# A cross-attention and quantised feed-forward kernel: GpSimd's additions wait for the affine passes, and the weight preparation moves from VectorE to ScalarE and GpSimd

## Chip, cores and metric

The kernel runs on one core of a Trainium2 chip. The metric is the device time of one execution, in microseconds. Engine names: PE or TensorE (matmuls), DVE or VectorE, ACT or ScalarE, POOL or GpSimd, SP or SyncE (DMA issue only here).

## What is computed

The input x is [64, 256, 256], the context [64, 120, 192], all float32. For each of the 64 blocks:

```python
x = x + xattn(layernorm(x), ctx, Wq, Wk, Wv, Wo, bo)      # 8 heads of 32
x = x + ffn(layernorm(x), ln1_g, ln1_b, w1, b1, ln2_g, ln2_b, w2, b2)

def ffn(x, ...):
    h = layernorm(x, ln1_g, ln1_b)
    h = bitlinear(h, w1, b1)          # 256 -> 1024
    h = gelu(h)
    h = layernorm(h, ln2_g, ln2_b)
    return bitlinear(h, w2, b2)       # 1024 -> 256

def act_quant_fake(x):                # per row
    scale = 127.0 / clip(max(abs(x), axis=-1), 1e-5)
    return clip(round(x * scale), -128, 127) / scale
def weight_quant_fake(w):             # per matrix
    scale = 1.0 / clip(mean(abs(w)), 1e-5)
    return clip(round(w * scale), -1, 1) / scale
def bitlinear(x, w, b):
    return act_quant_fake(x) @ weight_quant_fake(w).T + b
```

## The kernel before

The work has two stages over the same 64 blocks of 256 rows (NB = 64, two tiles of 128 rows each). The first does attention, the residual, the first feed-forward norm and its quantising, and keeps the quantised rows in SBUF. The second does the feed-forward part. Nothing of the second stage is changed.

Each engine has one program, written out by hand, and all follow the same step counter i. In the first stage a step of an engine is its function `attn(i, n)`, called by `steps`: steps from A0 = -5 up to L0 = 24 are straight code, those from 24 to 55 run in a hardware loop that holds four steps, the rest is straight again. After a straight step, and only there, `steps` calls what the table `aside` holds for it. Different parts of a step work on different blocks: the scores on block i, the values and sums on block i-1, the projection and the residual on i-2, the affine pass and the quantising on i-3.

What matters of a step, in each engine's own order:

- TensorE: scores (L1242), values (L1269), sums (L1278), first half of the projection (L1324), the turning of the score maxima (`turn_minima`, L1249), second half of the projection (L1324), `first_values` (L1288), the shift of the scores (L1255), `keys` (L1293 to L1298, behind x1_done), queries (L1314), `spread_inverses` (L1305).
- VectorE: the two affine passes of block i-3 (L702, `h = h * f_r + b1n_bc`, one for each row tile, both inputs in SBUF; then h_affine goes up), the transposing maximum of the scores in PSUM (L691, nm_part), the largest magnitude of h (L713), L718, L723, L729 (nm_t), the projection added to x (L735, x1_done), the reciprocals L739 (h_scaled) and L744, statistics (L749), L757 (inv_part), L762, the centring of h (L767, two) with f_ve between them (L771), the scaling of the queries (L779), the weighing of the output (L788). Its `aside` comes after L788.
- GpSimd: a wait for the scores of step i (raw_ps, released by L1242), the bias b2 added to xr of block i-3 (`add_b2`, L490), bo added to xr of block i-1 (`add_bo`, L485), three small operations of the input norm (L515, L517, and the power L520, which makes x_r), the quantising of block i-3 (`quantise`: L496 and twice L498, behind h_scaled), and the power L528 that makes f_r for the next affine passes (behind f_ve). Its `aside` comes after L528.
- ScalarE: copies of keys and values (L994, L996), a copy of the output (L977), four passes for the input statistics (L1009, L1013), the exponentials (L988), L982, and the cast of the quantised rows (L972). Its `aside` comes last.
- SP issues the DMAs in a fixed order, each behind the semaphore of what it needs: the turning of h (L382), ctx_t, xt, x_in, r_rows (behind r_done), xr, the store of xr (behind b2_done) and r_bc (behind the landed r_rows).

The weights are prepared in the same steps through `aside` (W_STEP = 4). SP loads w1 and w2 in eight pieces at steps 4 to 11. VectorE splits the bias b1 into three bf16 parts at steps 8 to 11 (`split_bias`: casts L655, subtractions L659, on one partition with 1024 elements), sums the magnitudes of the weights at steps 12 to 15 (`magnitude`, L635, four of 128x1024), makes mean and inverse at step 16 (L640 to L643, after TensorE's sum over partitions), and clamps at steps 18 to 21 (`clamp_weight`, L649, four of 128x1024). GpSimd rounds at steps 17 and 18 (`round_weight`, L463, two of 128x2048). ScalarE casts to bf16 at steps 19 to 22 (`place_weight`, L964, four of 128x1024). SP stores the bias parts at step 13 (`store_bias`, L355) and loads them back as rows at step 14 (`place_bias`, L361). At steps 57 and 58 VectorE inverts the scales of the quantised rows (`invert_scales`, L664, L666), and at steps 58 and 59 GpSimd splits them (`split_scales`).

## Time and profile before

| | us |
|---|---|
| median of 3 runs | 1240.67 |
| the runs | 1234.32, 1240.67, 1245.86 |
| the profiled execution's own time | 1247.94 |
| its span in the profile | 1246.3 |
| mean granted TensorE clock | 0.96 of full |

All durations below come from that one profiled execution. Its span runs from the first to the last instruction; the 1.6 us between it and the execution's own time lie around it. A line number stands for a line of the kernel before. Busy time of an engine counts instructions, not waiting; "idle before" is the time in which an engine had nothing to do ahead of an instruction, and the arrow names what released it. GpSimd's spans are rough, and the ends of matmuls are modelled. Steps are counted by the maximum L691, of which there is one for each block.

### The profile page before, as it was taken

Reading aid. Unit: us, or ns where it says so; the run is one execution under the profiler, and the core shown is the slowest. Engines: PE = TensorE matmul, PEld = TensorE weight load, DVE = VectorE, ACT = ScalarE, POOL = GpSimd, SP = SyncE. Lnnn points to the kernel's source line nnn. Section 1 sums busy time; section 2 is a strip of 40 time slices with the busy share of each in tenths; the row PEclk is TensorE's granted clock in tenths of the full one; section 3 lists DMA queues with packets and bytes.
Section 4 is the critical chain, followed back from the end, with each engine's and each line's share of the span. In section 5 each row is a group of like instructions: output and inputs, shape, how many; then the busy total and the mean of one; then the engine's idle time right before and its main releaser. Section 6 shows DMA issues by size and latency. Waiting matters only on the chain.

```text
span 1246.3 us, 29490 instructions
## 1 busy us (share of the span) xinstructions
PE 1007.4 (81%) x9649; PEld 671.1 (54%) x9649; DVE 1139.0 (91%) x1719; ACT 812.8 (65%) x2083; POOL 715.0 (57%) x924
## 2 busy tenths in 40 slices
PE   5988887888888888889888976777777777777776
PEld 4666655555666666666665643444444444444444
DVE  2799988889999999999999898999999999999997
ACT  4555544455545555555554447699999999999994
POOL 3355644545545555555555543767766766776776
PEclk8999988889999999999999887899999999999998
DMA  5467854445655655565656340032233223223224
GB/s 149 134 144 161 161 121 115 113 97 120 126 127 135 134 137 132 137 139 131 126 135 138 79 104 26 18 43 34 34 38 38 34 34 42 34 34 38 37 34 68
DMA packets 144472, 114.63 MB, mean 92 GB/s; under 512 B 51580, under 2 KB 134908, under 8 KB 144408
## 3 DMA queue, kind: packets, MB, share of 16 engines
q1 hardware_dynamic: 126824, 96.90, 34.4%
q0 software_dynamic: 16864, 16.26, 10.4%
q8 instruction: 36, 0.59, 0.2%
q10 hardware_dynamic: 720, 0.66, 0.2%
q14 instruction: 28, 0.23, 0.1%
HBM read 71.75 MB, written 33.63 MB: 85 GB/s over the span
## 4 chain that ended last, share of the span: by engine, by line
DVE 47%; PE 25%; issue 23%; POOL 3%; DVEq 1%; DMA 1%; ACT 0%; POOLq 0%; ACTq 0%
DVE nm_part L691 11%; PE banks L1314 10%; DVE h L702 8%; DVE gn_low L815 6%; DVE gn_high L815 6%; PE banks L1324 4%; PE banks L1293 4%; DVE o_t L788 3%; DVE xr L735 3%; DVE gn_high L801 2%; PE banks L1295 2%; POOL gn_high L541 1%; DVE gn_low L801 1%; DVE q_t L779 1%; PE banks L1297 1%
## 5 line engine op out<-in xcount | busy, mean ns | idle before, releaser
L988 ACT ACTIVATE probs<-banks 120x512 f32<-120x512 f32 x256 | 138.8, 598 | 206.2 <-PE banks L1255 206.2
L691 DVE TRANSPOSE_TENSOR_REDUCE nm_part<-banks 128x64 f16<-128x2048 f32 x64 | 147.4, 2304 | 4.7 <-PE banks L1242 4.6
L1324 PE MATMUL banks<-wo_sb,o_t 128*128 128x256 f32 x512 | 149.6, 418 | 0.9 <-DVE o_t L849 0.9
L1026 ACT ACTIVATE g_dev<-g,g_sum 128x1024 bf16<-128x1024 f32 x128 | 149.1, 1165 | 0.0
L1031 ACT ACTIVATE g<-banks,h_dq 128x1024 f32<-128x1024 f32 x128 | 142.5, 1131 | 7.4 <-PE banks L1189 7.4
L490 POOL TENSOR_TENSOR xr<-xr,b_bc 128x512 f32<-128x512 f32 x64 | 98.4, 1537 | 63.6 <-PE banks L1242 63.6
L1207 PE MATMUL banks<-w_t,g_t 128*128 128x256 bf16 x1008 | 123.2, 276 | 12.8 <-ACT g_t L1064 11.1
L1314 PE MATMUL banks<-xt,wq_c 128*128 128x256 f32 x512 | 130.6, 399 | 0.0
L1183 PE MATMUL banks<-w_t,h_t 128*128 128x512 bf16 x512 | 125.9, 390 | 1.9 <-ACT g L1031 1.3
L1207 PEld LDWEIGHTS banks<-w_t,g_t 128*128 128x128 f16 x1008 | 94.8, 99 | 51.4 <-issue 29.8
L702 DVE SCALAR_TENSOR_TENSOR h<-h,f_r,b1n_bc 128x256 f32<-128x256 f32 x122 | 115.8, 990 | 0.1
L528 POOL TENSOR_TENSOR f_r<-f_ve,neg_half 128x2 f32<-128x2 f32 x62 | 49.5, 798 | 110.6 <-DVE f_ve L771 110.6
L1314 PEld LDWEIGHTS banks<-xt,wq_c 128*128 128x128 f32 x512 | 94.0, 193 | 18.8 <-issue 0.9
L1324 PEld LDWEIGHTS banks<-wo_sb,o_t 128*128 128x128 f32 x512 | 91.2, 198 | 22.0 <-issue 14.0
L485 POOL TENSOR_TENSOR xr<-xr,bo_bc 128x512 f32<-128x512 f32 x64 | 91.5, 1430 | 17.0 <-DMA xr<-in_x 17.0
L496 POOL COPY h_dq<-h_cl 128x2 f32<-128x2 f32 (+1 forms) x64 | 13.9, 216 | 148.9 <-DVE h_qs L739 147.8
L561 POOL TENSOR_TENSOR g_r<-g_ve,neg_half 128x2 f32<-128x2 f32 x64 | 91.4, 1428 | 10.3 <-ACT g_ve L1047 10.3
L536 POOL TENSOR_TENSOR g_dq<-g_max,w_out 128x2 f32<-128x2 f32 x64 | 12.2, 190 | 146.1 <-DVE gn_low L815 85.7
L1249 PE MATMUL banks<-ident_h,nm_part 128*128 128x128 f16 x64 | 14.1, 221 | 95.2 <-DVE nm_part L691 95.2
L994 ACT ACTIVATE k_t<-banks 128x256 f32<-128x256 f32 x64 | 24.6, 385 | 99.9 <-DVE q_t L779 99.9
L1201 PE MATMUL banks<-ident_h,gn_low 128*128 128x128 f16 x512 | 42.0, 229 | 54.3 <-POOL gn_low L541 54.3
L801 DVE SCALAR_TENSOR_TENSOR gn_low<-g,g_nm,g_bc 128x1024 f32<-128x1024 f32 x64 | 81.3, 1277 | 0.0
(166 smaller groups left out, 2774.9 us busy)
## 6 DMA issues: line engine op xcount, KB each, us to landing
x_in<-in_x SPq DMA_DIRECT2D x64, 256.0 KB, 3.6
xt<-in_x_t SPq DMA_DIRECT2D x64, 256.0 KB, 3.5
xr<-in_x SPq DMA_DIRECT2D x64, 256.0 KB, 5.5
out<-xr SPq DMA_DIRECT2D x64, 256.0 KB, 5.7
out<-res POOLq DMA_DIRECT2D x62, 256.0 KB, 4.2
ctx_t<-in_ctx_t SPq DMA_DIRECT2D x64, 128.0 KB, 2.9
r_bc<-r_rows SPq DMA_DIRECT2D x64, 128.0 KB, 4.1
w_raw<-in_w_t SPq DMA_DIRECT2D x8, 256.0 KB, 5.2
```

Of the source, the lines that this page charges most:

```text
L490: pool.tensor_tensor(xr[:, r, :, :], xr[:, r, :, :], b2_bc[:, :].unsqueeze(1).to_broadcast([P, T, D]), ALU.add).then_inc(b2_done, 1)
L691: dve.tensor_reduce(nm_part[:, :, 0:C * RB], blocks_p, AX.X, ALU.max, negate=True, apply_transpose=True).then_inc(max_done, 1)
L702: last = dve.scalar_tensor_tensor(out=h[:, r1, t, :], in0=h[:, r1, t, :], scalar=f_r[:, q, t:t + 1], in1=b1n_bc[:, :], op0=ALU.mult, op1=A ...
L801: dve.scalar_tensor_tensor(out=gn[n][:, t, :], in0=g[:, p, t, :], scalar=g_nm[:, p, t:t + 1], in1=g2_bc[:, :], op0=ALU.add, op1=ALU.mult). ...
L815: dve.scalar_tensor_tensor(out=gn[n][:, t, :], in0=gn[n][:, t, :], scalar=g_r[:, p, t:t + 1], in1=b2n_bc[:, :], op0=ALU.mult, op1=ALU.add) ...
L988: act.activation(probs[:, p, j, :, :], sc_p[0:KV, j, :, :], ACT.Exp, scale=SCALE).then_inc(probs_done, 1)
L1026: act.activation(g_dev[:, t, :], g[:, p, t, :], ACT.Square, scale=-float(F), bias=g_sum[:, p, t:t + 1], accum_out=g_ssq[:, p, t:t + 1]).th ...
L1031: act.activation(g[:, p, t, :], u_p[t], ACT.Gelu, scale=h_dq[:, b, t:t + 1], accum_out=g_sum[:, p, t:t + 1]).then_inc(gelu_done, 1)
L1183: pe.matmul(u_p[t][:, cols], h_t[:, b, t * C + c, :], w1_t[:, c, cols], start=(c == 0), stop=False, skip_group_check=True)
L1207: pe.matmul(y[t], turned_rows[:, t, f, :], w2_t[:, f, :], start=(first and f == 0), stop=False, skip_group_check=True)
L1314: last = pe.matmul(q_p[:, m, :], wq_c[:, c, m * P:(m + 1) * P], xt[:, p, c, :], start=(c == 0), stop=(c == C - 1))
L1324: last = pe.matmul(y_p[:, t, :], o_t[:, p, c, t * P:(t + 1) * P], wo_sb[:, c, :], start=(c == 0), stop=(c == C - 1))
```

## The change

- On GpSimd, the wait for the scores at the head of a step is gone; `add_b2` of block i-3 now waits for h_affine of that block, which VectorE raises after the second pass L702.
- `magnitude` moves from VectorE to ScalarE, at the same steps 12 to 15: an Abs activation with a running sum. Its elementwise result goes to w1_t or w2_t, which `place_weight` writes over later.
- Rounding and clamping are both on GpSimd, in eight passes over 128x1024, alternating, one in each of the steps 18 to 25. They stand inside `attn`, between `quantise` and the power L528. `place_weight` comes at steps 20, 22, 24 and 26.
- The bias b1 lies on 128 partitions with 8 elements each for the split; its load and the three stores have pieces of 8 elements.
- L0, the first looped step, is 28.

```diff
@@ -285,8 +285,8 @@
         ctx_t = sb("ctx_t", [P, 2, 2, KP], scope=early_mem)
         w1_raw = sb("w1_raw", [P, C, F], scope=early_mem)
         w2_raw = sb("w2_raw", [P, FC, D], scope=early_mem)
-        b1_row = sb("b1_row", [1, F], scope=early_mem)
-        b1_part = sb("b1_part", [1, 3, F], BF16, scope=early_mem)
+        b1_cols = sb("b1_cols", [P, F // P], scope=early_mem)
+        b1_part = sb("b1_part", [P, 3, F // P], BF16, scope=early_mem)
         wq_sb = sb("wq_sb", [P, C, D], scope=early_mem)
         early_mem.close()
         ffn_mem = ctx.enter_context(ExitStack())
@@ -323,7 +323,7 @@
         biast_p = bank[3][:, 512 - P:512]
         u_p = [pair_a.rearrange("p a n -> p (a n)"), pair_b.rearrange("p a n -> p (a n)")]
 
-        A0, L0, L1 = -5, 24, NB - 5
+        A0, L0, L1 = -5, 28, NB - 5
         FFN_L0, FFN_L1, FFN_END = 8, NB - 3, NB + 3
         N_CONST = 7 + C * T
         SPLIT = (0, (NB - 12) // 2, NB - 12, NB)
@@ -341,7 +341,7 @@
                         sp.dma_start(dst[:, :], src.rearrange("(a n) -> a n", a=1).to_broadcast([P, D])).then_inc(rows_load, 16)
 
                 def load_bias():
-                    sp.dma_start(b1_row[:, :], b1.rearrange("(a n) -> a n", a=1)).then_inc(b1_load, 16)
+                    sp.dma_start(b1_cols[:, :], b1.rearrange("(p n) -> p n", p=P)).then_inc(b1_load, 16)
 
                 def load_weight(n):
                     part = slice(n % 4 * F * C // 4, (n % 4 + 1) * F * C // 4)
@@ -352,8 +352,8 @@
                 def store_bias():
                     sp.wait_ge(s_b1, 4)
                     for row, parts in ((0, 3), (3, 2), (5, 1)):
-                        sp.dma_start(b1_rows[row:row + parts].rearrange("(a r) n -> a (r n)", a=1),
-                                     b1_part[0:1, 0:parts, :].rearrange("a r n -> a (r n)")).then_inc(bias_stored, 16)
+                        sp.dma_start(b1_rows[row:row + parts].rearrange("r (p n) -> p r n", p=P),
+                                     b1_part[:, 0:parts, :]).then_inc(bias_stored, 16)
 
                 def place_bias():
                     sp.wait_ge(bias_stored, 16 * 3)
@@ -457,10 +457,23 @@
                 def bias_here():
                     pool.wait_ge(s_load, 16 * 2)
 
-                def round_weight(m):
-                    raw = (w1_raw, w2_raw)[m]
+                def weight_part(n):
+                    m, part = n // 2, n % 2
+                    raw = (w1_raw, w2_raw)[m][:, :, :].rearrange("p a n -> p (a n)")[:, part * C * F // 2:(part + 1) * C * F // 2]
+                    return m, raw
+
+                def round_weight(n):
+                    m, raw = weight_part(n)
                     pool.wait_ge(mean_done, 2)
-                    pool.tensor_scalar(raw[:, :, :], raw[:, :, :], w_inv[:, m:m + 1], MAGIC, ALU.mult, ALU.add).then_inc(w_rounded, 1)
+                    pool.tensor_scalar(raw, raw, w_inv[:, m:m + 1], MAGIC, ALU.mult, ALU.add).then_inc(w_rounded, 1)
+
+                def clamp_weight(n):
+                    m, raw = weight_part(n)
+                    pool.wait_ge(w_rounded, n + 1)
+                    pool.tensor_scalar(raw, raw, MAGIC + 1.0, MAGIC - 1.0, ALU.min, ALU.max).then_inc(w_clamped, 1)
+
+                weight_steps = {W_STEP + 14 + 2 * n: (lambda n=n: round_weight(n)) for n in range(4)}
+                weight_steps.update({W_STEP + 15 + 2 * n: (lambda n=n: clamp_weight(n)) for n in range(4)})
 
                 def split_scales(m):
                     v = slice(SPLIT[m], SPLIT[m + 1])
@@ -478,7 +491,6 @@
                     pool.tensor_copy(bias_row[:, v, :, 5], h_res2[:, v, :]).then_inc(split_chain, 1)
 
                 aside = {-1: bias_here, 1: lambda: pool.wait_ge(rows_load, 16 * 3), NB - 6: lambda: split_scales(0), NB - 5: lambda: split_scales(1)}
-                aside.update({W_STEP + 13 + n: (lambda n=n: round_weight(n)) for n in range(2)})
 
                 def add_bo(b, r):
                     pool.wait_ge(xr_loaded[r], (b - r) * 4 + 16)
@@ -501,10 +513,9 @@
 
                 def attn(i, n):
                     p, q = n % 2, 1 - n % 2
-                    if live(i, NB) and live(i - 1, NB):
-                        pool.wait_ge(raw_ps, i + 1)
                     b = i - 3
                     if live(b, NB):
+                        pool.wait_ge(h_affine, b + 1)
                         add_b2(b, (n + 1) % 4)
                     b = i - 1
                     if live(b, NB):
@@ -521,6 +532,8 @@
                     b = i - 3
                     if live(b, NB):
                         quantise(b, (n + 1) % 4)
+                    if isinstance(i, int) and i in weight_steps:
+                        weight_steps[i]()
                     b = i - 2
                     if live(b, NB):
                         after(pool, h_affine, b - 1)
@@ -628,13 +641,6 @@
                 def rows_here():
                     dve.wait_ge(rows_load, 16 * 3)
 
-                def magnitude(n):
-                    m, part = n // 2, n % 2
-                    dve.wait_ge(w_load, 16 * 8)
-                    w = (w1_raw, w2_raw)[m][:, :, :].rearrange("p a n -> p (a n)")
-                    dve.tensor_reduce(w_abs[:, part, m:m + 1], w[:, part * C * F // 2:(part + 1) * C * F // 2], AX.X, ALU.add,
-                                      apply_absolute_value=True).then_inc(mag_done, 1)
-
                 def mean_magnitude():
                     dve.wait_ge(mag_sum, 1)
                     dve.tensor_scalar(w_mean[:, :], bank[1][:, 0:2], 1.0 / (F * D), CLIP, ALU.mult, ALU.max).then_inc(mean_done, 1)
@@ -642,21 +648,15 @@
                     dve.reciprocal(w_inv[:, :], w_mean[:, :]).then_inc(mean_done, 1)
                     dve.tensor_scalar(w_out[:, :], w_mean[:, 1:2], 1.0 / QMAX, None, ALU.mult).then_inc(w_out_done, 1)
 
-                def clamp_weight(n):
-                    m, part = n // 2, n % 2
-                    raw = (w1_raw, w2_raw)[m][:, :, :].rearrange("p a n -> p (a n)")[:, part * C * F // 2:(part + 1) * C * F // 2]
-                    dve.wait_ge(w_rounded, m + 1)
-                    dve.tensor_scalar(raw, raw, MAGIC - 1.0, MAGIC + 1.0, ALU.max, ALU.min).then_inc(w_clamped, 1)
-
                 def split_bias(n):
                     if n % 2 == 0:
                         after(dve, s_b1, n)
                         dve.wait_ge(b1_load, 16)
-                        dve.tensor_copy(b1_part[:, n // 2, :], b1_row[:, :]).then_inc(s_b1, 1)
+                        dve.tensor_copy(b1_part[:, n // 2, :], b1_cols[:, :]).then_inc(s_b1, 1)
                     else:
                         dve.wait_ge(s_b1, n)
-                        dst = b1_row[:, :] if n == 1 else b1_part[:, 2, :]
-                        dve.tensor_tensor(dst, b1_row[:, :], b1_part[:, n // 2, :], ALU.subtract).then_inc(s_b1, 1)
+                        dst = b1_cols[:, :] if n == 1 else b1_part[:, 2, :]
+                        dve.tensor_tensor(dst, b1_cols[:, :], b1_part[:, n // 2, :], ALU.subtract).then_inc(s_b1, 1)
 
                 def invert_scales(n):
                     v = slice(SPLIT[n], SPLIT[n + 1])
@@ -681,8 +681,6 @@
 
                 aside = {1: rows_here, W_STEP + 12: mean_magnitude,
                          NB - 7: lambda: invert_scales(0), NB - 6: lambda: invert_scales(1)}
-                aside.update({W_STEP + 8 + n: (lambda n=n: magnitude(n)) for n in range(4)})
-                aside.update({W_STEP + 14 + n: (lambda n=n: clamp_weight(n)) for n in range(4)})
                 aside.update({W_STEP + 4 + n: (lambda n=n: split_bias(n)) for n in range(4)})
 
                 def largest(b):
@@ -964,7 +962,16 @@
                     act.activation(wt[:, :, :].rearrange("p a n -> p (a n)")[:, cols],
                                    raw[:, :, :].rearrange("p a n -> p (a n)")[:, cols], ACT.Copy, bias=-MAGIC).then_inc(tern_done, 1)
 
-                aside = {W_STEP + 15 + n: (lambda n=n: place_weight(n)) for n in range(4)}
+                def magnitude(n):
+                    m, part = n // 2, n % 2
+                    raw, wt = ((w1_raw, w1_t), (w2_raw, w2_t))[m]
+                    cols = slice(part * C * F // 2, (part + 1) * C * F // 2)
+                    act.wait_ge(w_load, 16 * 8)
+                    act.activation(wt[:, :, :].rearrange("p a n -> p (a n)")[:, cols], raw[:, :, :].rearrange("p a n -> p (a n)")[:, cols],
+                                   ACT.Abs, accum_out=w_abs[:, part, m:m + 1]).then_inc(mag_done, 1)
+
+                aside = {W_STEP + 8 + n: (lambda n=n: magnitude(n)) for n in range(4)}
+                aside.update({W_STEP + 16 + 2 * n: (lambda n=n: place_weight(n)) for n in range(4)})
 
                 def cast_rows(b, r):
                     act.wait_ge(hq_done, b + 1)
```

## Rows read from the trace of the kernel before

**Rows 1.** The page: busy times, and the granted clock in 40 slices.
```profile
PE 1007.4 (81%) x9649; PEld 671.1 (54%) x9649; DVE 1139.0 (91%) x1719; ACT 812.8 (65%) x2083; POOL 715.0 (57%) x924
...
PEclk8999988889999999999999887899999999999998
```

**Rows 2.** Timeline, one step: start us, us, engine, line, operation, [idle before <-releaser].
```profile
396.81 2.30 DVE L691 TRANSPOSE_TENSOR_REDUCE nm_part<-banks 128x64 f16<-128x2048 f32 x1
...
401.61 0.94 POOL L498 TENSOR_SCALAR h<-h,h_qs 128x256 f32<-128x256 f32 x2
...
402.52 1.99 PE L1314 MATMUL banks<-xt,wq_c 128*128 128x256 f32 x8
402.85 0.35 DVE L757 SCALAR_TENSOR_TENSOR inv_part<-inv_hi,part_sign,inv_sum 128x128 f16<-128x128 f16 x1
...
404.11 0.85 POOL L528 TENSOR_TENSOR f_r<-f_ve,neg_half 128x2 f32<-128x2 f32 x1 [1.56 <-DVE f_ve L771]
...
404.56 0.69 DVE L779 TENSOR_TENSOR q_t<-banks,r_bc 128x512 f32<-128x512 f32 x1
...
405.76 1.90 DVE L702 SCALAR_TENSOR_TENSOR h<-h,f_r,b1n_bc 128x256 f32<-128x256 f32 x2
405.93 1.45 POOL L490 TENSOR_TENSOR xr<-xr,b_bc 128x512 f32<-128x512 f32 x1 [0.97 <-PE banks L1242]
...
407.58 2.30 DVE L691 TRANSPOSE_TENSOR_REDUCE nm_part<-banks 128x64 f16<-128x2048 f32 x1
...
410.03 0.22 PE L1249 MATMUL banks<-ident_h,nm_part 128*128 128x128 f16 x1 [1.28 <-DVE nm_part L691]
```

**Rows 3.** Timeline, step 9 to step 10, with the bias split.
```profile
117.39 0.86 DVE L702 SCALAR_TENSOR_TENSOR h<-h,f_r,b1n_bc 128x256 f32<-128x256 f32 x2
...
118.18 2.30 DVE L691 TRANSPOSE_TENSOR_REDUCE nm_part<-banks 128x64 f16<-128x2048 f32 x1
...
120.62 0.22 PE L1249 MATMUL banks<-ident_h,nm_part 128*128 128x128 f16 x1 [0.94 <-DVE nm_part L691]
...
127.22 1.20 DVE L659 TENSOR_TENSOR b_row<-b_row,b_part 1x1024 f32<-1x1024 f32 x1
...
129.15 2.30 DVE L691 TRANSPOSE_TENSOR_REDUCE nm_part<-banks 128x64 f16<-128x2048 f32 x1
```

**Rows 4.** Timeline of steps with long idle time; windows (PE busy, clock, DMA, GB/s).
```profile
165.02 0.27 PE L1249 MATMUL banks<-ident_h,nm_part 128*128 128x128 f16 x1 [2.52 <-DVE nm_part L691]
...
268.02 2.91 DVE L702 SCALAR_TENSOR_TENSOR h<-h,f_r,b1n_bc 128x256 f32<-128x256 f32 x2
...
697.08 0.27 PE L1249 MATMUL banks<-ident_h,nm_part 128*128 128x128 f16 x1 [2.53 <-DVE nm_part L691]
...
271.00:285.00 14.00, 10.91 (x105) 0.88 0.43 109
```

**Rows 5.** Timeline, VectorE: the maximum L691 of step 3 and of step 63.
```profile
53.34 2.30 DVE L691 TRANSPOSE_TENSOR_REDUCE nm_part<-banks 128x64 f16<-128x2048 f32 x1
...
738.35 2.32 DVE L691 TRANSPOSE_TENSOR_REDUCE nm_part<-banks 128x64 f16<-128x2048 f32 x1 [1.49 <-PE banks L1242]
```

**Rows 6.** Timeline, step 60.
```profile
706.14 1.27 POOL L490 TENSOR_TENSOR xr<-xr,b_bc 128x512 f32<-128x512 f32 x1
...
709.14 0.71 POOL L520 TENSOR_TENSOR x_r<-x_ve,neg_half 128x2 f32<-128x2 f32 x1
709.19 0.43 DVE L729 TENSOR_TENSOR nm_t<-nm_row,block_sel 128x256 f16<-128x256 f16 x1
```

**Rows 7.** Groups by shape, whole run: xcount | busy us, mean ns | idle before.
```profile
L635 DVE TENSOR_REDUCE w_abs<-w_raw 128x1 f32<-128x1024 f32 x4 | 4.8, 1209 | 0.0
...
L964 ACT ACTIVATE w_t<-w_raw 128x1024 bf16<-128x1024 f32 x4 | 4.3, 1076 | 0.0
L463 POOL TENSOR_SCALAR w_raw<-w_raw,w_inv 128x2048 f32<-128x2048 f32 x2 | 3.9, 1967 | 0.0
...
L1009 ACT ACT_TABLE_LOAD x1 | 1.3, 1283 | 3.6 <-issue 3.6
```

## The prediction

> **What bounds the kernel now.** I read the page first, to split the run by stage. GpSimd and ScalarE are busy for 57% and 65% of the span and VectorE for 91%, and TensorE's granted clock is full nearly everywhere [rows 1]. All edits lie in the attention stage or its set-up, so I took one of its steps in order of time, then the same piece of it under other conditions.
>
> One step at full clock [rows 2]: once VectorE has added the projection (L735), TensorE does keys and queries, and its last query matmul ends at 402.52 + 1.99 = 404.51; VectorE scales the queries at 404.56 (L779), then weighs the output, then runs the two affine passes L702 (1.90 us for both), then the transposing maximum L691 (2.30), for which TensorE waits 1.28 us at L1249. So two engines take turns: one piece belongs to TensorE (L735 to L779), the rest to VectorE, and L702 stands on the path. GpSimd's add L490 starts at 405.93, while L702 runs.
>
> Steps whose L702 is not overlapped in this way stand in the same trace, in the four steps where VectorE has a piece of the bias split ahead of it [rows 3]: the pair takes 0.86, and L691 starts 118.18 - 117.39 = 0.79 us after it, against 407.58 - 405.76 = 1.82 in rows 2. In these steps TensorE idles only 0.94 us before L1249. The step from 118.18 to 129.15 is 10.97 long, of which 1.20 is the subtraction L659: a clean step takes 9.77.
>
> From rows 2, worked the other way: the usual step there is 407.58 - 396.81 = 10.77, less 1.82 - 0.79 = 1.03, is 9.74. I take 9.78 for all.
>
> There is a second price. Where VectorE is later still, both of GpSimd's additions fall on L702: in [rows 4] the pair takes 2.91 us, where it usually takes 1.90. TensorE then idles longer before L1249: 2.3 to 3.9 us in 12 steps (the first and the last of them stand in the rows), elsewhere at most 1.5. In each of the 12 the granted clock falls to the lower of its two levels (1.2 GHz) for some microseconds; 0.88 is a mean over such a step. L691 starts at 53.34 in step 3 and at 738.35 in the last, step 63 [rows 5]: the 60 steps between take 685.0 us. At 10.8 for the usual 48, the 12 have (685.0 - 518.4) / 12 = 13.9 each.
>
> **The change, part by part.** The profiled execution took 1247.94 us for a span of 1246.3. It lies 7.3 above the median of the runs shown; the sum is made against it.
>
> 1. GpSimd's add L490 waits for the affine passes in place of the scores. VectorE, from L779 on, loses 1.03 us per step. What is late next? TensorE: its 1.28 idle before L1249 shrinks to about 0.25, so it just doesn't take over, and with the idle time gone there is no reason left for the clock to fall. Sum: 60 steps x 9.78 = 586.8 in place of 685.0, that is 98.2 less; one more L702 pair before 53.34 gives 1.0. This counts the side work of all these steps as gone; what comes back is added below.
>
> Behind the new wait on GpSimd stand L490, the add L485, the three small operations of the input norm, the quantising and the power L528. They start 0.9 later. A step of the trace has that very order [rows 6]: L490 starts at 706.14, when the affine passes are over, and takes 1.27 (not 1.45); the power L520 ends at 709.85, and VectorE's L729 and what follows are on time. L490 and L485 then lie beside L691, which reads PSUM, and the start of the reduction L713; neither was longer there. The quantising needs h_scaled, which VectorE makes after that, so it is no later. The r_rows store, the xr load and the xr store on SP come some 0.3 later within the step; each has over 1 us to spare.
>
> In that step L520 runs from 709.14 to 709.85 and L729, which has two SBUF inputs, starts at 709.19 and takes its usual 0.43. The Trainium skill (SBUF — State Buffer, "SBUF: two separate sides") says that a GpSimd operation and a VectorE operation with two SBUF inputs take a shared port as an exclusive lock for the whole instruction. By that rule L729 would have stood until 709.85, 0.66 late. The row shows otherwise for this small operation, though for the long additions the same rule fits L702.
>
> 2. Weight magnitudes leave VectorE: four of 1.21 [rows 7]. On ScalarE each costs about 1.08 as the like pass L964, plus an accumulator read. It stands after the step's last copy, with over 1.3 us until ScalarE's next work, the key copy behind L779. Bounds: 0 to 2.6 a piece more, if Abs wanted a table of its own and Exp had to be loaded back (1.28 each, L1009), of which little would reach the path; I take 0. TensorE's sum waits for all four one step after the last, as before.
>
> 3. Rounding (2 x 1.97 on GpSimd) and clamping (four passes on VectorE) become eight GpSimd passes over 1024 elements, one in each of the steps 18 to 25, between quantising and L528. A rounding of 2048 took 1.97, so half of it is 1.0 to 1.1. Clamping on GpSimd is not in the trace: bounds 0.9 (as rounding) to 2.0; I take 1.1. In rows 2 the quantising ends at 401.61 + 0.94 = 402.55, so the pass lies from about 402.6 to 403.7, on VectorE's L757 (402.85, two SBUF inputs). If that has to wait for the end, VectorE is 0.8 late, less the 0.14 that it now waits for L779: 0.7 a step, 8 x 0.7 = 5.6. Bounds: 0, if L757 starts first, and 1.7 x 8 = 13.6. TensorE's idle time becomes about 0.9, far below 2.3. L528 isn't late: it starts at 404.11, when the pass is over.
>
> 4. The bias split on 128 partitions: two casts and two subtractions (1.20 each in rows 3) over 1024 elements of one row become four operations over 8. The nearest in rows is the smallest two-input one, L757 with 0.35 over 128 elements; so 0 to 1.4 for the four, and I take 0.5. The load and the three stores now have pieces of 16 to 32 bytes, 768 in the stores. SP waits for the stores a step later (place_bias); nothing of this step needs the bias before the second stage. 0, at worst a few us once.
>
> 5. What stays on VectorE's path: the mean at step 16 (three small operations and a wait for TensorE, 0.5), the inversions of scales in two steps (0.7 each), and GpSimd's scale split, whose pieces still meet L702 (0.6 in all): 2.5.
>
> 6. The straight part is four steps longer (24 to 28): straight steps are at most 0.1 longer than looped ones. 0.
>
> Sum: -98.2 - 1.0 + 5.6 + 0.5 + 2.5 = -90.6. 1247.94 - 90.6 = 1157.3; the second stage isn't touched. I predict 1157. The clean steps are absolute lengths, so I don't take the 7.3 to the median off: what differed between runs is probably how many steps lost the clock, and those are replaced.
>
> **The rivals.**
> - TensorE takes over. Its margin is 0.25 a step, and the modelled ends of matmuls may hide that it is already used up. For: L779 already waits for it. Against: rows 3, a clean pair with TensorE still idle. At 10.2 a step 60 x 0.42 = 25 more: 1182. Chance 5%.
> - Small GpSimd operations do block L729: 0.66 x 60 = 40 more, 1197. Against: rows 6. Beside it stands the lock rule told above. Chance 4%.
> - The weight passes cost the clock: clamping near its upper bound, both L757 and L767 held back, TensorE idle over 2.3, eight steps of 13.9 (worked out above). 8 x (13.9 - 10.5) = 27 more: 1184. For: this stretch did it before. Against: each pass is half as long and no addition is on L702 any more. Chance 6%.
> - The wait doesn't part the two (the additions meet other VectorE work that is as dear). Then only VectorE's side work goes, about 12 (4 x 1.21, the clamps as much, the split 3): 1236. Rows 6 speak against it. Chance 3%.
> - Slower: GpSimd's late row becomes the bound. If its work between the affine pass and L528 grew so that f_r came late to L702, VectorE would stand in each step, TensorE would idle beyond 2.3 and stay at 1.2 GHz: 60 steps at 13.9 are 834, 149 more than now, 1397. It decides from 0.8 us, the time between L528's end (404.96) and L702 in rows 2. Against: GpSimd's own work in a step is about 6 of 9.8 us, and it waits for VectorE twice in it. Chance 3%.
>
> The forecast has 79%, with a range of its own from 1148 to 1168. The whole range, 1143 to 1190, takes in the first and third rival and the bounds of part 3, and a few us for the second stage. A measurement here can tell about 1% from no change (1228 to 1253). Faster 0.94, same 0.03, slower 0.03.
>
> **What would show it.** L702 at 0.43 to 0.48 each, L490 at 1.27 and starting within 0.2 of L691; L691 every 9.7 to 9.8; TensorE's wait before L1249 near 0.25 and never over 2; full clock from the fourth step on; steps 18 to 25 about 0.7 longer, with L757 late. Wrong would be steps over 10.2 at full clock with VectorE waiting for L1314 (first rival), L729 longer than 0.43 (second), granted clock below 1 near step 20 (third), VectorE idle ahead of L702 (last).

## The result and the profile after

The changed kernel takes 1157.59 us (median of 4 runs, 1156.48 to 1161.56), the kernel before beside it 1241.9. The ratio is 0.9334, with a 95% interval from 0.9283 to 0.9384. The profiled execution took 1157.24 for a span of 1155.6, 90.7 less than the profiled execution before by either number; 90.6 was forecast. Between the medians it is 84.3, mostly because the profiled execution before was 6 us above its median.

The page of the changed kernel, the lines of [rows 1]:

```profile
PE 984.1 (85%) x9649; PEld 655.4 (57%) x9649; DVE 1070.7 (93%) x1711; ACT 815.4 (71%) x2091; POOL 711.5 (62%) x930
...
PEclk8999999999999999999999888999999999999998
```

TensorE is idle less, and its clock is full in the attention stage from the second slice on. VectorE has 68 us less of busy time. The three stretches, cut at L691 of step 3 and of the last step (L689 in the changed kernel), first before, then after. Columns: us, then busy time and count of PE, PEld, DVE, ACT and POOL, then the granted clock, the DMA share and GB/s:

```profile
0.00:53.34 53.34, 39.56 (x356) 28.46 (x356) 22.38 (x46) 25.85 (x85) 19.23 (x42) 0.94 0.52 139
53.34:738.35 685.01, 583.75 (x6251) 413.17 (x6252) 630.31 (x1219) 346.13 (x997) 359.27 (x546) 0.96 0.58 128
738.35:1246.30 507.95, 384.10 (x3050) 229.45 (x3042) 486.27 (x455) 440.77 (x1002) 336.46 (x338) 0.96 0.28 39
```

```profile
0.00:51.90 51.90, 37.53 (x325) 26.89 (x329) 21.35 (x46) 25.09 (x83) 17.04 (x40) 0.93 0.52 143
51.90:649.93 598.03, 563.07 (x6284) 400.38 (x6280) 563.00 (x1212) 350.68 (x1006) 344.98 (x553) 1.00 0.69 146
649.93:1155.60 505.67, 383.53 (x3050) 228.18 (x3043) 486.33 (x455) 439.61 (x1002) 349.47 (x338) 0.96 0.30 39
```

87.0 of the 90.7 us were saved in the 60 steps, 1.4 ahead of them and 2.3 behind; that last stretch varies as much between runs (504.0 to 508.0 in the traces of this case). The clock of the steps rose from 0.96 to 1.00. In the timeline, one looped step (L700, L689, L502 and L1256 are L702, L691, L490 and L1249 of before; further down, L721, L727, L733, L755, L765 and L777 are L723, L729, L735, L757, L767 and L779):

```profile
560.21 2.31 DVE L689 TRANSPOSE_TENSOR_REDUCE nm_part<-banks 128x64 f16<-128x2048 f32 x1
...
562.67 0.22 PE L1256 MATMUL banks<-ident_h,nm_part 128*128 128x128 f16 x1 [0.25 <-DVE nm_part L689]
...
569.17 0.87 DVE L700 SCALAR_TENSOR_TENSOR h<-h,f_r,b1n_bc 128x256 f32<-128x256 f32 x2
...
569.96 2.31 DVE L689 TRANSPOSE_TENSOR_REDUCE nm_part<-banks 128x64 f16<-128x2048 f32 x1
...
570.12 1.27 POOL L502 TENSOR_TENSOR xr<-xr,b_bc 128x512 f32<-128x512 f32 x1 [1.75 <-DVE h L700]
```

From L689 at 560.21 to the next at 569.96 the step takes 9.75, where [rows 2] have 10.77. The pair of affine passes takes 0.87 and not 1.90. GpSimd's addition follows 0.16 after the start of the maximum and takes 1.27. TensorE waits 0.25 where it waited 1.28. The group of L700, against 990 ns a pass before:

```profile
L700 DVE SCALAR_TENSOR_TENSOR h<-h,f_r,b1n_bc 128x256 f32<-128x256 f32 x122 | 53.2, 477 | 0.4 <-POOL f_r L541 0.2
```

Where the changed kernel is not at its clean length, three things stand in its trace. First, a weight pass of GpSimd (step 19 to 20):

```profile
222.55 1.04 POOL L473 TENSOR_SCALAR w_raw<-w_raw 128x1024 f32<-128x1024 f32 x1
...
222.89 0.83 DVE L755 SCALAR_TENSOR_TENSOR inv_part<-inv_hi,part_sign,inv_sum 128x128 f16<-128x128 f16 x1
```

L755 usually takes 0.35. Here it ends at 223.72, just after the pass that began at 222.55 (223.59): 0.48 lost on VectorE. The step is 10.01 long, the clean straight one 9.85.

Second, in steps 10 to 18 transfers were late. SP's issues and GpSimd's addition L497 in step 15, the longest one (12.55):

```profile
171.85 0.47 SPq L378 DMA_DIRECT2D r_rows<-x_r  x1
...
172.36 0.43 SPq L408 DMA_DIRECT2D xr<-in_x  x1
...
178.96 0.34 SPq L416 DMA_DIRECT2D r_bc<-r_rows  x1
...
180.54 1.27 POOL L497 TENSOR_TENSOR xr<-xr,bo_bc 128x512 f32<-128x512 f32 x1 [5.84 <-DMA xr<-in_x]
```

r_rows is issued at 171.85, and what waits for its landing, r_bc, only at 178.96. The load of xr, issued at 172.36, lets L497 start at 180.54, after 5.84 of waiting. From 120 to 200 SP stood 39.8 us in all for r_rows, in 8 waits of at most 6.7.

Third, steps 57 and 58, with the inversions, take 10.43 and 10.59.

The step lengths of all kernels, as means over stretches, worked out from the starts of the transposing maximum. "steps" is the sum from 3 to 62:

```
                     3-7    8-11  12-17  18-25  28-55  57-59   steps
before              10.88  10.71  12.76  12.80  10.82  13.26   685.0
changed              9.85  10.08  10.80  10.09   9.75  10.35   598.0
changed, again       9.85   9.93  10.11  10.04   9.75  10.35   594.3
wait alone           9.85  10.71  10.80  10.28   9.75  10.35   602.5
old wait            10.88  13.46  11.36  12.08  10.77  12.64   677.4
SP order             9.85   9.93   9.96  10.02   9.75  10.36   592.8
before + 0.1        12.90  11.17  13.25  12.95  10.84  13.55   707.5
before + 0.3        13.15  12.95  13.57  13.72  13.44  13.12   801.8
changed + 0.6       10.52  10.61  10.50  10.59  10.35  10.83   627.8
changed + 2.2       13.48  13.48  13.72  13.62  13.29  13.78   806.5
behind the maximum  10.12  10.19  10.39  10.60  10.01  10.53   611.5
one affine pass      9.45   9.64   9.99   9.69   9.41   9.90   574.8
```

### The profile page after: what moved, and what is told of

Read it like the earlier page. It is cut to its first block, busy times and chain, and to the rows that moved or that the text cites. A ratio compares the mean times of both kernels' runs of the same rounds, so it can differ in the third digit from the quotient of the medians.

```text
span 1155.6 us, 29367 instructions
## 1 busy us (share of the span) xinstructions
PE 984.1 (85%) x9649; PEld 655.4 (57%) x9649; DVE 1070.7 (93%) x1711; ACT 815.4 (71%) x2091; POOL 711.5 (62%) x930
## 4 chain that ended last, share of the span: by engine, by line
DVE 43%; issue 25%; PE 21%; DMA 6%; SPq 3%; POOL 1%; DVEq 1%; ACT 1%; POOLq 0%; ACTq 0%
DVE nm_part L689 10%; PE banks L1321 9%; DVE gn_low L813 7%; DVE gn_high L813 7%; DMA r_rows<-x_r 5%; PE banks L1300 3%; DVE xr L733 3%; DVE h L700 3%; DVE o_t L786 2%; PE banks L1331 2%; DVE gn_low L799 2%; DVE gn_high L799 2%; PE banks L1302 1%; DVE h_max L711 1%; DVE g_max L819 1%
## 5 line engine op out<-in xcount | busy, mean ns | idle before, releaser
L689 DVE TRANSPOSE_TENSOR_REDUCE nm_part<-banks 128x64 f16<-128x2048 f32 x64 | 147.8, 2309 | 3.7 <-PE banks L1249 3.7
L502 POOL TENSOR_TENSOR xr<-xr,b_bc 128x512 f32<-128x512 f32 x64 | 82.6, 1290 | 102.2 <-DVE h L700 100.4
L1331 PE MATMUL banks<-wo_sb,o_t 128*128 128x256 f32 x512 | 140.8, 398 | 1.1 <-DVE o_t L847 1.0
L574 POOL TENSOR_TENSOR g_r<-g_ve,neg_half 128x2 f32<-128x2 f32 x64 | 104.5, 1633 | 8.6 <-ACT g_ve L1054 8.6
L497 POOL TENSOR_TENSOR xr<-xr,bo_bc 128x512 f32<-128x512 f32 x64 | 81.1, 1266 | 39.3 <-DMA xr<-in_x 39.1
L1331 PEld LDWEIGHTS banks<-wo_sb,o_t 128*128 128x128 f32 x512 | 86.9, 189 | 21.0 <-issue 14.1
L799 DVE SCALAR_TENSOR_TENSOR gn_high<-g,g_nm,g_bc 128x1024 f32<-128x1024 f32 x64 | 80.9, 1271 | 0.0
L813 DVE SCALAR_TENSOR_TENSOR gn_low<-gn_low,g_r,b2n_bc 128x1024 f32<-128x1024 f32 x64 | 79.2, 1279 | 0.0
L1249 PE MATMUL banks<-q_t,k_t 32*128 32x256 f32 x1024 | 75.0, 407 | 4.9 <-ACT k_t L1001 4.8
```

Source lines behind the costliest of these rows:

```text
L502: pool.tensor_tensor(xr[:, r, :, :], xr[:, r, :, :], b2_bc[:, :].unsqueeze(1).to_broadcast([P, T, D]), ALU.add).then_inc(b2_done, 1)
L574: pool.tensor_tensor(g_r[:, q, :], g_ve[:, q, :], neg_half[:, 0:T], ALU.pow).then_inc(gr_done, 1)
L689: dve.tensor_reduce(nm_part[:, :, 0:C * RB], blocks_p, AX.X, ALU.max, negate=True, apply_transpose=True).then_inc(max_done, 1)
L799: dve.scalar_tensor_tensor(out=gn[n][:, t, :], in0=g[:, p, t, :], scalar=g_nm[:, p, t:t + 1], in1=g2_bc[:, :], op0=ALU.add, op1=ALU.mult). ...
L813: dve.scalar_tensor_tensor(out=gn[n][:, t, :], in0=gn[n][:, t, :], scalar=g_r[:, p, t:t + 1], in1=b2n_bc[:, :], op0=ALU.mult, op1=ALU.add) ...
L1331: last = pe.matmul(y_p[:, t, :], o_t[:, p, c, t * P:(t + 1) * P], wo_sb[:, c, :], start=(c == 0), stop=(c == C - 1))
```

## The experiments

### The wait alone

```diff
--- kernel before
-                    if live(i, NB) and live(i - 1, NB):
-                        pool.wait_ge(raw_ps, i + 1)
                     b = i - 3
                     if live(b, NB):
+                        pool.wait_ge(h_affine, b + 1)
                         add_b2(b, (n + 1) % 4)
```

> The kernel before with one edit: add_b2 waits for h_affine, the scores' wait goes. Theory (the affine passes run alone, and the lower clock came only from additions that met them): steps of 9.75 to 9.85 us plus VectorE's own side work, 3.7 for the bias split, 4 x 1.15 for magnitudes, 4 x 0.7 for clamps, so 1157 + 11 less a few us: 1154 to 1168 us, TensorE's wait ahead of its turning of the maxima under 2 us everywhere. Rival (moving the side work is what cured the steps at the lower clock): those steps stay, 12 x 3.1 more: 1190 or above.

Measured: 1163.51 us, ratio 0.9382 (0.9339 to 0.9426). A step with a magnitude sum on VectorE (columns as in the timelines above):

```profile
164.09 1.21 DVE L634 TENSOR_REDUCE w_abs<-w_raw 128x1 f32<-128x1024 f32 x1
...
165.22 0.87 DVE L701 SCALAR_TENSOR_TENSOR h<-h,f_r,b1n_bc 128x256 f32<-128x256 f32 x2
...
168.46 0.22 PE L1248 MATMUL banks<-ident_h,nm_part 128*128 128x128 f16 x1 [1.48 <-DVE nm_part L690]
```

VectorE's 1.21 stand ahead of the passes, which take 0.87 all the same. TensorE waits 1.48 and keeps its clock; the step is 10.97 long, 1.12 over a clean one. Before, such steps took 12.0 to 13.5. No step from 3 to 61 of this trace is below full clock. So the wait alone cures the steps at the lower clock, and the rival falls.

### The changed kernel with the old wait

```diff
--- changed kernel
+                    if live(i, NB) and live(i - 1, NB):
+                        pool.wait_ge(raw_ps, i + 1)
                     b = i - 3
                     if live(b, NB):
-                        pool.wait_ge(h_affine, b + 1)
                         add_b2(b, (n + 1) % 4)
```

> The changed kernel with GpSimd's old wait for the scores back, all else as changed. Theory: each of 60 steps pays 1.03 again, 1157 + 62 = 1219, and since VectorE has no side work any more, few steps or none have TensorE idle beyond 2.3 us: 1210 to 1225. Rival (the lower clock comes from the overlap alone): 12 steps at 13.9 are back as well, 1235 to 1250. Other rival (the wait does nothing, the side work did it): 1157.

Measured: 1235.72 us, ratio 0.9957 (0.9931 to 0.9983). All edits but the wait are worth some 4 us by themselves. I had 1210 to 1225: the small operations that are left on VectorE were not harmless. The time lies in the range of the first rival (1235 to 1250), but not with the rival's steps: steps 13 and 14 are usual ones here, and 8 to 11 and several of 18 to 25 are the long ones, with 9 steps at the lower clock. Step 8, with a cast of the bias over 8 elements:

```profile
116.59 0.16 DVE L656 CAST b_part<-b_cols 128x8 bf16<-128x8 f32 x1
116.66 1.28 POOL L502 TENSOR_TENSOR xr<-xr,b_bc 128x512 f32<-128x512 f32 x1 [0.96 <-PE banks L1250]
116.66 2.97 DVE L701 SCALAR_TENSOR_TENSOR h<-h,f_r,b1n_bc 128x256 f32<-128x256 f32 x2
...
117.90 1.45 POOL L497 TENSOR_TENSOR xr<-xr,bo_bc 128x512 f32<-128x512 f32 x1
...
122.01 0.22 PE L1257 MATMUL banks<-ident_h,nm_part 128*128 128x128 f16 x1 [2.52 <-DVE nm_part L690]
```

The cast takes 0.16, and for that GpSimd's L502 is no longer behind VectorE's first pass. The pair now takes 2.97, and TensorE waits 2.52. Steps 9 to 11 take 13.4 to 15.0, steps 18 to 25 with their weight passes 12.1. This gave a sharper theory: the price hangs on which of the two starts first. If VectorE does (0.07 to 0.25 ahead in the usual steps of before), its first pass runs, the second stands until the addition ends: 1.90. If GpSimd does, the first pass stands for L502 and the second one for L497, and the pair ends 2.97 after L502 began. That makes 2.9 where both start together. In steps 12 to 15 of before the addition began 1.06 ahead, beside a magnitude sum; the pair took 1.92 and ended 2.98 after it.

Steps 8 to 11 of before look like an exception, since L490's record begins 0.5 to 1.1 ahead of L702 there and the pair is clean [rows 3]. Two more rows of that step:

```profile
116.79 0.67 DVE L655 CAST b_part<-b_row 1x1024 bf16<-1x1024 f32 x1
116.86 2.53 POOL L490 TENSOR_TENSOR xr<-xr,b_bc 128x512 f32<-128x512 f32 x1 [0.97 <-PE banks L1242]
```

VectorE's cast began 0.07 ahead of L490, and L490 lasts until 119.39, 1.14 after the passes: it took 2.53 in place of 1.27, so here GpSimd stood and VectorE paid nothing. So VectorE's operation of that moment counts, and not only L702: a long cast ahead of the addition held it back, the magnitude sum (a tensor_reduce) didn't. The next two experiments tried the order.

### The kernel before with 0.1 us more on VectorE

```diff
--- kernel before, in attn of VectorE, behind L788
+                    if live(i - 3, NB) and live(i, NB):
+                        dve.tensor_scalar(spare[:, :], ones[:, 0:2], 1.0, None, ALU.mult)
```

> The kernel before with one more VectorE operation over 128x2 elements (about 0.1 us) between the weighing of the output and the affine passes, in all steps from 3 on. Theory: which of L702 and L490 starts first decides. In the kernel before VectorE is first by 0.1 to 0.2 us and pays 1.03; made later by 0.1 to 0.16 it finds L490 running, waits for it, and L485 then falls on the second pass: the pair takes 2.9, a step 12.0 or more, TensorE stands 2.4 us and may lose its clock: 1240 + 60 x 1.2 = 1312 or more, up to 1430. Rival (the price is a share of the common path and grows with the overlap, not with the order): 0.1 a step, 1246.

Measured: 1268.55 us, ratio 1.0241 (1.0208 to 1.0273). Here L703 and L491 are L702 and L490 of before. A straight step, then a looped one:

```profile
75.22 0.16 DVE L791 TENSOR_SCALAR spare<-ones 128x2 f32<-128x2 f32 x1
75.29 2.98 DVE L703 SCALAR_TENSOR_TENSOR h<-h,f_r,b1n_bc 128x256 f32<-128x256 f32 x2
75.29 1.28 POOL L491 TENSOR_TENSOR xr<-xr,b_bc 128x512 f32<-128x512 f32 x1 [1.67 <-PE banks L1245]
```

```profile
429.92 0.16 DVE L791 TENSOR_SCALAR spare<-ones 128x2 f32<-128x2 f32 x1
429.99 1.90 DVE L703 SCALAR_TENSOR_TENSOR h<-h,f_r,b1n_bc 128x256 f32<-128x256 f32 x2
430.09 1.52 POOL L491 TENSOR_TENSOR xr<-xr,b_bc 128x512 f32<-128x512 f32 x1 [0.96 <-PE banks L1245]
```

The extra operation costs VectorE 0.07. In the straight steps, where it was ahead by about as much, both start together and the pair takes 2.98; steps 4 to 6 take 13.3 to 13.4 where they took 10.88. In the loop, VectorE was ahead by 0.17 and still is by 0.10: the pair takes 1.90, and a step is 0.07 longer. My figure of 1312 or more was a miss, since I had counted the looped steps in; both kinds do what the order says. The order can't be read to the last hundredth: in the looped step 27 of before L702 begins 0.05 ahead by the profile, and the pair takes 3.02.

### The same with 0.3 us

```diff
--- kernel before, in attn of VectorE, behind L788
+                    if live(i - 3, NB) and live(i, NB):
+                        dve.tensor_reduce(spare[:, :], wo_sb[:, 0, :], AX.X, ALU.max)
```

> As the small extra operation on the kernel before, but a reduction over 256 elements (about 0.25 to 0.3 us of VectorE), longer than the 0.17 by which L702 is ahead of L490 in the looped steps. Theory (the order of these two decides): now the looped steps tip over as well, pair 2.9 or more, TensorE standing 2.4 to 2.6, 12.0 a step at full clock and 13.4 where it falls: 1240 + 60 x (13.2 - 11.4) = 1348, 1320 to 1370. Rival (the looped steps can't tip): 11.1 a step in the loop, 1268 + 32 x 0.25 = 1276.

Measured: 1365.14 us, ratio 1.1002 (1.0890 to 1.1115).

```profile
440.14 0.41 DVE L791 TENSOR_REDUCE spare<-wo_sb 128x1 f32<-128x256 f32 x1
...
440.39 1.28 POOL L491 TENSOR_TENSOR xr<-xr,b_bc 128x512 f32<-128x512 f32 x1 [1.10 <-PE banks L1245]
440.47 2.90 DVE L703 SCALAR_TENSOR_TENSOR h<-h,f_r,b1n_bc 128x256 f32<-128x256 f32 x2
...
441.63 1.46 POOL L486 TENSOR_TENSOR xr<-xr,bo_bc 128x512 f32<-128x512 f32 x1
...
445.74 0.22 PE L1252 MATMUL banks<-ident_h,nm_part 128*128 128x128 f16 x1 [2.61 <-DVE nm_part L692]
```

Columns of the next one: us, PE busy (count), granted clock, DMA share, GB/s, over steps of the loop:

```profile
300.00:800.00 500.00, 404.85 (x3898) 0.87 0.46 108
```

Now the loop has turned too: L491 starts 0.08 ahead of L703 (0.16 in most steps), both additions fall on the passes, TensorE waits 2.61. A looped step takes 13.44 in place of 10.82: some 0.3 us of work cost 2.6. The rival (1276) falls.

### The changed kernel with 0.6 us and with 2.2 us more

```diff
--- changed kernel, in attn of VectorE, behind L786; n = 1 and n = 4
+                    if live(i - 3, NB) and live(i, NB):
+                        dve.tensor_reduce(spare[:, :], wo_sb[:, :, :].rearrange("p c n -> p (c n)").unsqueeze(1).to_broadcast([P, n, C * D]), AX.XY, ALU.max)
```

> The changed kernel with a reduction over 512 elements (0.57 us more of VectorE) in each step ahead of the affine passes. Theory (with the additions behind the passes, a delay of VectorE costs its own length and no more, and TensorE's wait of 0.8 to 0.9 doesn't touch the clock): 10.32 in the loop and 10.42 outside, 1154 + 34 = 1188. Rival (any delay still tips something): 1210 or more.

> The changed kernel with a VectorE reduction over 2048 elements more in each step, ahead of the affine passes; nothing overlaps them. Theory (TensorE standing for about 2.4 us loses its full clock whatever made it stand): 9.75 + 2.2 + 1.3 = 13.2 to 13.5 a step, granted clock 0.85 to 0.9, 1153 + 60 x 3.6 = 1369, 1350 to 1400. Rival (the lower clock in the kernel before had another cause): 12.0 a step at full clock, 1153 + 60 x 2.2 = 1285.

Measured: 1186.96 us with 0.6 (ratio 0.9566, 0.9501 to 0.9632) and 1363.01 with 2.2 (ratio 1.0996, 1.0953 to 1.1040); 1188 and 1369 were forecast. With 0.6:

```profile
438.38 0.68 DVE L789 TENSOR_REDUCE spare<-wo_sb 128x1 f32<-128x512 f32 x1
438.98 0.87 DVE L701 SCALAR_TENSOR_TENSOR h<-h,f_r,b1n_bc 128x256 f32<-128x256 f32 x2
...
442.22 0.22 PE L1259 MATMUL banks<-ident_h,nm_part 128*128 128x128 f16 x1 [0.85 <-DVE nm_part L690]
```

TensorE waits 0.85 and the loop takes 10.35, which is 9.75 and the 0.60 of the reduction: nothing turns over. With 2.2:

```profile
431.54 0.87 DVE L701 SCALAR_TENSOR_TENSOR h<-h,f_r,b1n_bc 128x256 f32<-128x256 f32 x2
...
434.78 0.22 PE L1259 MATMUL banks<-ident_h,nm_part 128*128 128x128 f16 x1 [2.45 <-DVE nm_part L690]
...
437.24 1.22 PE L1303 MATMUL banks<-ctx_t,w_kv 128*128 128x128 f32 x4
```

```profile
300.00:800.00 500.00, 407.98 (x3913) 0.87 0.49 108
```

The pair L701 is clean (0.87). TensorE has stood for 2.45 nevertheless and then runs at the lower clock (1.2 GHz): its L1303 takes 1.22, at full clock 0.71, and the granted clock is 0.87 over the loop. A looped step takes 13.29, which is 9.75 + 2.2 + 1.3. So the lower clock follows TensorE's standing still, and it needs no overlap with the additions. Waits ahead of the turning of the maxima of up to 1.5 left it alone in every trace of this case. Of the 158 waits of 2.2 or more, 149 were followed by a step below full clock; the other 9 weren't, as three steps here (a wait of 2.45, a length of 11.95) and three with the old wait. In between lie only four waits, which went both ways.

### The additions behind the maximum

```diff
--- changed kernel
                         pool.wait_ge(h_affine, b + 1)
+                        if live(i, NB):
+                            pool.wait_ge(max_done, i + 1)
                         add_b2(b, (n + 1) % 4)
```

> The changed kernel with add_b2 waiting for the transposing maximum as well, so that the additions start about 2.3 us later. Theory (a VectorE operation with two SBUF inputs stands until a running GpSimd addition has ended): L727, at 3.17 after the maximum's start, stands until 3.7, and GpSimd's later quantising meets the two-input passes L755 and L765: 0.5 to 1.5 a step, 1183 to 1243. Rival (only affine passes are touchy): 1153 to 1158.

Measured: 1171.32 us, ratio 0.945 (0.9413 to 0.9487). The rival falls, but a step lost 0.27 and not 0.5 or more. What stood wasn't what I had named (L723 and L729 are L721 and L727 of the changed kernel):

```profile
433.01 0.64 DVE L713 TENSOR_REDUCE h_max<-h 128x2 f32<-128x512 f32 x1
433.17 1.27 POOL L502 TENSOR_TENSOR xr<-xr,b_bc 128x512 f32<-128x512 f32 x1 [3.79 <-DVE nm_part L691]
...
433.77 0.69 DVE L723 TENSOR_SCALAR h_cl<-h_max 128x2 f32<-128x2 f32 x1
```

It is L723, h_cl, over 128x2 elements with one SBUF input: 0.69 in place of 0.16, until 434.46, when L502 has ended (434.44). Only 0.24 of it reaches L735, which waits for TensorE anyway. In step 16 of the changed kernel, where the addition is late, L721 is caught in the same way (0.91). The other price that I had named, quantising against L757 and L767, was 0.1 to 0.2 on one L767, and hidden. The Trainium skill (SBUF — State Buffer, "Who interferes with whom") has tensor_scalar among the operations that can, with the right operands, enter a two-port mode and so contend with GpSimd, and tensor_reduce as one that never does; by that rule this row agrees, and so does L713, which ran 0.64 beside the same addition.

### One affine pass left out

```diff
--- changed kernel
-                        for t in range(T):
+                        for t in range(T - 1):
                             last = dve.scalar_tensor_tensor(out=h[:, r1, t, :], in0=h[:, r1, t, :],
```

> The changed kernel with the second of the two affine passes of each step left out (row tile 1 keeps the centred values). Theory (VectorE and TensorE are nearly level, with 0.25 us of TensorE's wait left): a step gets 0.25 shorter, not 0.43: 9.5, 1153 - 15 = 1138, TensorE's wait before its turning of the maxima near 0. Rival (VectorE alone is the bound): 9.32 a step, 1127.

Measured: 1135.16 us, ratio 0.9158 (0.9119 to 0.9197).

```profile
435.59 0.47 DVE L700 SCALAR_TENSOR_TENSOR h<-h,f_r,b1n_bc 128x256 f32<-128x256 f32 x1
...
437.45 1.13 PE L1331 MATMUL banks<-wo_sb,o_t 128*128 128x256 f32 x4
438.44 0.22 PE L1256 MATMUL banks<-ident_h,nm_part 128*128 128x128 f16 x1
```

A clean step takes 9.35 in the loop: 0.40 less, nearly the 0.43 of the rival, with no wait of TensorE left. So VectorE was the bound of the changed kernel, and TensorE had some 0.4 us a step to spare, not the 0.25 that its wait showed. The rows say where the rest was: L1256 starts at 438.44, 0.14 before the modelled end of L1331 (438.58), so that end is too late by that much at least, and 0.25 + 0.14 is 0.39. The two engines are now about level. The total stands in between, as some steps of this run had late transfers (steps 15 and 31: 11.05 and 10.12).

### SP's order, and the changed kernel again

```diff
--- changed kernel, in attn of SP
-                    b = i - 5
-                    if live(b, NB):
-                        turn_rows(b, (n + 3) % 4)
...
+                    b = i - 4
+                    if live(b, NB):
+                        turn_rows(b, n % 4)
                     b = i + 3
                     if live(b, NB):
                         sp.wait_ge(r_stored[q], (b - q) * 8 + 16)
```

> The changed kernel with SP's transposing load of h for the next step put ahead of the wait for the landed r_rows, instead of behind it. The changed kernel has steps of 10.5 to 12.6 us between steps 10 and 18, in which SP stands 5.5 to 8.4 us for r_rows. Theory (SP's row of waits is the bound in those steps): each pass of SP's row gets 1.2 shorter, most of the 7 us that these steps lose goes: 1150 to 1154. Rival (the landing of xr itself is late, whatever SP's order): 1156 to 1159.

> The changed kernel once more, beside the others: 1157, with 1155 to 1161 for its single runs.

Measured, side by side: 1152.10 us for the new order (ratio 0.9285, 0.9252 to 0.9318) and 1152.69 for the changed kernel again (0.9288, 0.9255 to 0.9321). No difference. Both lie in the 1150 to 1154 that the theory gave, which therefore speaks for nothing, and the repeated kernel (single runs 1150.45 to 1154.22) is below the 1155 to 1161 that I had for it. SP's waits from 120 to 200, first in the changed kernel again, then with the new order:

```profile
SPq L416 <- DMA r_rows<-x_r: 35.2, 8, 6.5
```

```profile
SPq L378 <- POOL x_r L531: 18.7, 7, 3.5
SPq L382 <- ACT hq L979: 13.0, 8, 2.0
SPq L416 <- DMA r_rows<-x_r: 3.2, 3, 2.0
```

The waits for the landed r_rows went from 35.2 to 3.2 us, but SP now stands for GpSimd's x_r and ScalarE's hq: 34.9 us in all, where the changed kernel again has 37.2 with all its waits. And in this set of runs the steps 12 to 17 of the changed kernel took 10.11 on average, and not 10.80 as in the first profile, so there was hardly anything to win. SP has room for its wait, unless the landings themselves are late. Why the first runs had 4 to 5 us more of them is open; the program was the same. Whether the new stores of the bias, in 768 pieces, have a share in it wasn't tested either. Step 15 takes 10.20 in both kernels here, 0.35 over a clean one, while in the run with the wait alone, which stores the bias from one row, it is as long as the steps before it (10.98 and 10.97).

## Why the prediction was right

- **What bounds the kernel.** That VectorE and TensorE take turns, that L702 stands on the path, and that a clean step lasts 9.75 to 9.78: borne out, with 9.75 in the loop and 9.85 outside. The straight steps are 0.1 longer in both kernels; 28 x 9.75 + 32 x 9.85 = 588.2 against the 586.8 that I had. The 9.77 read from [rows 3] was low for a straight step: I took off L659's full 1.20, and its start is only 1.14 ahead of L702's.
- **Part 1, the wait.** The size was right, 76 of the 87 us by the run with the wait alone. The mechanism was put too simply: a pass that is overlapped pays 1.03, and one that comes "later still" pays for both additions. What sets the price is who starts first, and the usual step before was 0.07 to 0.25 us from paying twice that. It is why the sum over 60 steps, and not the usual step, had to be taken, which the prediction did, with the lower clock as its second price. It put that price on the 12 steps in which TensorE idled; the trace has 16 steps over 11 us, as a step behind a long wait is long too. The sum isn't touched by that.
- **Part 1, what stands behind the new wait.** On time, as the order in [rows 6] had shown. L727 takes 0.43 to 0.46, as before or nearly; by the Trainium skill's rule (SBUF — State Buffer, "SBUF: two separate sides"), as the prediction cites it, L727 would have stood for L531, and that didn't happen. "Over 1 us to spare" on SP was wrong for steps 10 to 18: in the profile late transfers cost some 6 us there, in a later run under 2. I had put 0.
- **Part 2, magnitudes to ScalarE.** 0 on the path, as put, for three of the four: in the later run, steps 12 to 14 took 9.85. Step 15, with the fourth, took 10.20; ScalarE then waits for VectorE, so it isn't ScalarE's pass that is late, and what is wasn't found. ScalarE needed 1.06 and 0.20 a piece. On VectorE they would have cost 1.12 a step, as the run with the wait alone shows.
- **Part 3, the eight passes.** Mis-sized: 5.6 forecast, 8 x 0.16 = 1.3 measured. The pass does hold L755, for 0.48 (not 0.8, as it starts before L755 would, at 222.55), and VectorE had 0.3 to spare before L777, not 0.14; that was read from a looped step, while these are straight ones. Rounding took 1.16 and clamping 1.04, near the 1.1 taken.
- **Part 4, the bias split.** 4 x 0.08 = 0.3 against 0.5. With the split on one partition, steps 8 to 11 take 10.71 and not 9.93.
- **Part 5.** Mean, inversions, splits: steps 57 to 59 are 1.5 over clean ones, of 2.0 forecast; the mean's 0.5 can't be told from step 16's late transfer in the profile, but with the wait alone and with SP's new order step 16 is 10.17, so it is 0.3.
- **The sum.** It came out at 1157 partly by luck: the passes were 4 too dear, the transfers some 6 too cheap, the clean steps 1.4 too short, and the ends of the stage gave 2.7 more than the 1.0 that I had. The same program took 1152.7 in the later set. That I left the 7.3 to the median in fits the runs: of 17 later executions of the kernel before, those near 1248 have a granted clock of 0.963, those near 1237 0.968 to 0.971.
- **The rivals.** TensorE doesn't take over, and had more room than its wait showed. Small GpSimd operations don't block L729, but a long one does block a tiny tensor_scalar. The passes didn't cost the clock. The two did part. VectorE's idle time ahead of L700 is 0.4 us in all.

The edits aren't additive. The wait alone is worth 76 us, the rest alone 4, both 87: without the wait, every small operation that remains on VectorE, and every pass on GpSimd that delays L755, can turn the order over. That the additions, and not some other work of GpSimd behind the same wait, are what the passes stand for is read from the rows (most long pairs end 0.28 after an addition does); no run took the additions out.

## What to carry to other kernels

When two engines meet on a shared resource, look which one starts first and by how much. A lead of 0.1 us can hide a price twice as high, so a wait that fixes the order was worth more here than the overlap it gave up. Sum over all steps, not the usual one: here the 16 of 60 steps that were over 11 us gave about half of the 87 us, because side work delayed VectorE in them, and in most TensorE then stood for over 2.2 us and ran at its lower clock. Steps in which side work happens to put two instructions apart show beforehand what a change that parts them will give.

## What was unexpected of the hardware

- An operation of 0.07 us on VectorE made a step 2.5 us longer (10.88 to 13.4), through the order of the two additions and then the clock.
- A VectorE tensor_scalar over 2 elements of a partition stood 0.53 us for a GpSimd addition (0.69 in place of 0.16), though it has one SBUF input; the two-input L727 didn't stand for GpSimd's power over 2 elements that ran at the same time.
- TensorE's wait of 0.25 before L1256 was not its whole room: leaving out 0.43 of VectorE's work made the step 0.40 shorter.
- A cast on one partition that began 0.07 us ahead of GpSimd's addition held the addition back until two further VectorE passes were done (2.53 in place of 1.27); a tensor_reduce in the same place didn't.
